# Centring the first expert weights during the first image steps, with the loads of both expert weights in the other order

## The reference

```python
x = x + _L0_conv_ref(_ln_c(x), ...)      # per image: a 3x3 convolution whose taps depend on the image
t = _to_tokens(x)
t = t + _L0_ffn_ref(_ln_t(t), ...)
...
def _L0_ffn_ref(x, Wg, bg, W1, b1, W2, b2):
    gate_logits = xf @ Wg + bg
    top_w, top_i = jax.lax.top_k(gate_logits, 2)
    ...
    for e in range(E):
        h = jax.nn.gelu(xf @ W1[e] + b1[e], approximate=False)
        out = out + w_dense[:, e:e + 1] * (h @ W2[e] + b2[e])
```

## Time and profile before

| | |
|---|---|
| median of three runs | 1544.35 us |
| the profiled execution | 1543.75 us, of which the span from first to last instruction is 1541.5 us |
| busy share of the span | TensorE 94%, VectorE 86%, ScalarE 71%, GpSimd 63% |
| first phase, up to the choice of the last pair | 0 to 570 us |
| turn between the phases | 570 to 611 us |
| second phase | 611 to 1541 us |
| granted TensorE clock, mean | 0.961 of full speed |

### The profile page before, as it was taken

The page is one execution under the profiler, slowest core; times in us unless marked ns, Lnnn a source line. Parts: engine busy times, 40 slices in busy tenths (PEclk is TensorE's granted clock), DMA queues, the critical chain, the costliest instruction groups (busy, mean ns, idle before and its releaser), DMA issues.

```text
span 1541.5 us, 45757 instructions
## 1 busy us (share of the span) xinstructions
PE 1446.2 (94%) x12204; PEld 1114.9 (72%) x12205; DVE 1326.2 (86%) x2693; ACT 1096.8 (71%) x2514; POOL 973.6 (63%) x1057
## 2 busy tenths in 40 slices
PE   5899999999999848999999999999999999999996
PEld 2345444454545422999999999999999999999995
DVE  2568888888888885999999999989999999999995
ACT  4577777777777622777777777777777777777773
POOL 1004455554555476577777777777777777777773
PEclk7899999999999955999999999999999999999998
DMA  4201212121222026111111223222322222222223
GB/s 140 82 28 57 69 62 79 64 74 56 73 69 65 31 83 138 47 45 43 44 40 55 68 86 92 88 93 86 92 86 91 86 91 86 90 81 82 75 78 108
DMA packets 85647, 115.77 MB, mean 75 GB/s; under 512 B 17613, under 2 KB 69865, under 8 KB 85590
## 3 DMA queue, kind: packets, MB, share of 16 engines
q1 hardware_dynamic: 64886, 76.83, 16.9%
q0 software_dynamic: 18112, 34.27, 6.8%
q10 hardware_dynamic: 2592, 4.00, 0.9%
HBM read 60.08 MB, written 58.48 MB: 77 GB/s over the span
## 4 chain that ended last, share of the span: by engine, by line
POOL 36%; PE 25%; issue 25%; ACT 8%; DVE 2%; POOLq 2%; DMA 1%; SPq 0%; DVEq 0%; ACTq 0%
POOL token_out L532 15%; POOL xn L520 13%; PE psV L860 12%; POOL yt L527 8%; PE psV L811 4%; ACT spent L628 3%; PE psT L845 2%; PE psA L802 2%; PE psG L847 2%; ACT cv L616 1%; ACT sq L584 1%; DMA stage<-in_L_ffn_W_dram 1%; POOLq L532 1%; DVE x L1174 1%; ACT lnv L591 1%
## 5 line engine op out<-in xcount | busy, mean ns | idle before, releaser
L1390 DVE TENSOR_TENSOR gl<-g,gh 128x512 f16<-128x512 f32 x620 | 497.6, 841 | 62.4 <-ACT gh L739 54.8
L502 POOL DMA_INDIRECT rows_by_pair<-rows,idx x256 | 269.2, 1052 | 325.4 <-issue 201.9
L532 POOL DMA_INDIRECT token_out<-yt,rt x310 | 354.5, 1144 | 185.0 <-POOL yt L527 132.7
L860 PE MATMUL psV<-lp,diag 128*128 128x512 f32 x576 | 275.1, 610 | 18.7 <-ACT cv L616 17.6
L739 ACT ACTIVATE gh<-g 128x512 f16<-128x512 f32 x465 | 274.5, 624 | 16.9
L732 ACT ACTIVATE g<-psT 128x512 f32<-128x512 f32 x310 | 182.0, 597 | 100.9 <-PE psT L996 61.0
L732 ACT ACTIVATE g<-psV 128x512 f32<-128x512 f32 x310 | 184.8, 598 | 90.1 <-PE psV L996 68.7
L520 POOL TENSOR_SCALAR xn<-rt 128x128 f32<-128x128 f32 x310 | 217.1, 709 | 9.4 <-DMA rt<-rows_by_pair 5.6
L1017 PE MATMUL psR<-wall,gh 128*128 x1240 | 221.3, 273 | 0.4 <-DVE ya L1407 0.4
L1017 PE MATMUL psG<-wall,gh 128*128 x1240 | 221.3, 273 | 0.0
L1018 PE MATMUL psG<-wall,gl 128*128 x1240 | 213.0, 219 | 0.0
(11 more groups left out here) (224 smaller groups left out, 2958.5 us busy)
## 6 DMA issues: line engine op xcount, KB each, us to landing
rt<-rows_by_pair SPq DMA_DIRECT2D x155, 133.0 KB
xb<-in_x_dram SPq DMA_DIRECT2D x32, 512.0 KB, 3.4
yq<-token_out SPq DMA_DIRECT2D x112, 128.0 KB, 2.3
out_dram<-oq SPq DMA_DIRECT2D x112, 128.0 KB
token_out<-yt,rt POOLq DMA_INDIRECT x310
rows_by_pair<-rows,idx POOLq DMA_INDIRECT x256, 2.4
stage<-in_L_ffn_W_dram SPq DMA_DIRECT2D x1, 2048.0 KB, 8.8
ye<-token_out SPq DMA_DIRECT2D x4, 512.0 KB, 4.1
```

The source lines that it names most:

```text
L502: gp.indirect_dma_start(rows_dram, bass.IndirectOffsetOnAxis(ap=idx[p][:, b:b + 1].bitcast(U32), axis=0), rows[p][:, b, :], None).then_inc ...
L532: gp.indirect_dma_start(y_dram, bass.IndirectOffsetOnAxis(ap=rt[r][:, b, ID:ID + 1].bitcast(U32), axis=0), yt[r][:, b, :], None, bounds_ch ...
L860: ins = te.matmul(psConv.rearrange("p (h w) -> p h w", w=WW), diag[k][:, m, :], lp[j][:, y:y + HH // 2, dx:dx + WW], start=(m == 0), stop= ...
L1390: v.tensor_tensor(gl[side][q][:, cols], g[side][:, cols], gh[side][q][:, cols], ALU.subtract).then_inc(lo_done, 1)
```

## The change

The loads change places, and W1 is made ready during the image steps:

- SP loads W1 at the place of W2's load; the wait and the load behind it are gone.
- TensorE multiplies W1 with `centre_w` (the identity less the mean) in place of the ones, so that the bank holds the centred weights, and adds b1 / 128 with the same second matmul. There are three banks (both halves of `psT` and `psG`); an expert from the fourth on waits until the bank's low part is read. Experts 0 to 2 stand at the end of step 0, 3 to 5 in the middle of step 1, 6 and 7 at the end of step 1.
- ScalarE makes the high part from the bank (three experts and b2 in the first half of step 1, three after the second square of step 1, two at the start of step 2), then issues the load of W2.
- VectorE makes the low part from the bank (three after the first norm of step 1, three before the second, two in step 2 after the first window taps).
- `turn` of step 2, which uses `psT` and `psG`, waits until all eight low parts are made.
- W2 is split by ScalarE in step 3 (four experts in the middle, four at its end) and by VectorE at the ends of steps 3 and 4. `low_b2` moves from step 0 to the end of step 1.
- The shift products, the shift, the high and the low parts between the phases are gone.

```diff
@@ SP
-            sp.dma_start(stage_2, W2.rearrange("e (s p) d -> p e s d", p=P)).then_inc(s_stage, 16)
+            sp.dma_start(stage_1, W1.rearrange("e d h -> d e h")).then_inc(s_stage, 16)
...
-            sp.wait_ge(s_low, 1)
-            sp.dma_start(stage_1, W1.rearrange("e d h -> d e h")).then_inc(s_stage, 16)
@@ ScalarE
+            def high_w1(part):
+
+                for e in range(*W1_PARTS[part]):
+                    act.wait_ge(s_w1_centred, e + 1)
+                    sc_.activation(wall_e[:, e, O_1H:O_1L], w1_bank[e % 3], ACT.Copy, scale=WSCALE).then_inc(s_w1_high, 1)
...
+                if st_.is_step(2):
+                    high_w1(2)
+                    act.dma_start(stage_2, W2.rearrange("e (s p) d -> p e s d", p=P)).then_inc(s_stage, 16)
                 if st_.on(2):
                     diagonals(st_, 0)
...
-                    if st_.first and k == 1:
-                        high_w2(E - 2, E)
+                    if k == 0 and st_.is_step(1):
+                        high_b2()
+                        high_w1(0)
                     if st_.on(1):
                         inv_std(st_, k, 1)
...
-                    if st_.first and k == 1:
-                        high_b2()
...
-                    if st_.first and k == 0:
-                        high_w2(0, E // 2)
                     if st_.on(1):
                         if k == 0:
                             square(st_, 1)
-                    if st_.first and k == 0:
-                        high_w2(E // 2, E - 2)
+                    if k == 0 and st_.is_step(1):
+                        high_w1(1)
+                    if k == 0 and st_.is_step(3):
+                        high_w2(0, E // 2)
                 if st_.next().on(1):
                     square(st_.next(), 0)
+                if st_.is_step(3):
+                    high_w2(E // 2, E)
...
-            for e in range(E):
-                act.wait_ge(s_shifted, e + 1)
-                sc_.activation(wall_e[:, e, O_1H:O_1L], stage_1[:, e, :], ACT.Copy, scale=WSCALE).then_inc(s_high, 1)
@@ TensorE
+            def centre_w1(part):
+
+                if part == 0:
+                    pe.wait_ge(s_stage, 16)
+                    pe.wait_ge(s_b1, 1)
+                for e in range(*W1_PARTS[part]):
+                    if e >= 3:
+                        pe.wait_ge(s_w1_low, e - 2)
+                    te.matmul(w1_bank[e % 3], centre_w[:, :], stage_1[:, e, :], start=True, stop=False)
+                    te.matmul(w1_bank[e % 3], ident[0:E, e:e + 1].broadcast_to([E, P]), b1n[:, :], start=False, stop=True).then_inc(s_w1_centred, 1)
...
                 pe.wait_ge(x1_ready, st_.count(3, 2, k + 1))
+                if k == 0 and st_.is_step(2):
+                    pe.wait_ge(s_w1_low, E)
...
+                    if k == 0 and st_.is_step(1):
+                        centre_w1(1)
...
+                for part, at in ((0, 0), (2, 1)):
+                    if st_.is_step(at):
+                        centre_w1(part)
...
-            for e in range(E):
-                te.matmul(shift_bank[e], ones[:, :], stage_1[:, e, :], start=True, stop=False)
-                te.matmul(shift_bank[e], ident[0:E, e:e + 1].broadcast_to([E, P]), b1n[:, :], start=False, stop=True).then_inc(s_shift, 1)
-
             pe.wait_ge(tab_ready, 2)
-            pe.wait_ge(s_shifted, 2)
...
-            pe.wait_ge(s_low, 2 + E)
+            pe.wait_ge(s_low, 2)
@@ VectorE
+            def low_w1(part):
+
+                for e in range(*W1_PARTS[part]):
+                    dve.wait_ge(s_w1_high, e + 1)
+                    v.scalar_tensor_tensor(out=wall_e[:, e, O_1L:O_2], in0=w1_bank[e % 3], scalar=WSCALE, in1=wall_e[:, e, O_1H:O_1L], op0=ALU.mult, op1=ALU.subtract).then_inc(s_w1_low, 1)
...
+                if st_.is_step(2):
+                    low_w1(2)
                 if st_.on(1):
                     norm(st_, 0)
...
-                    low_w2(0, E // 2)
+                if st_.is_step(1):
+                    low_w1(0)
...
                     window(st_, 2, 0, 0, 3)
+                if st_.is_step(1):
+                    low_w1(1)
                 if st_.on(1):
                     norm(st_, 1)
...
                     add_image(st_, 1)
-                if st_.first:
+                if st_.is_step(1):
+                    low_b2()
+                if st_.is_step(3):
+                    low_w2(0, E // 2)
+                if st_.is_step(4):
                     low_w2(E // 2, E)
-                    low_b2()
...
-            for e in range(E):
-                dve.wait_ge(s_shift, e + 1)
-                v.scalar_tensor_tensor(out=stage_1[:, e, :], in0=shift_bank[e], scalar=-1.0 / D, in1=stage_1[:, e, :], op0=ALU.mult, op1=ALU.add).then_inc(s_shifted, 1)
...
-            for e in range(E):
-                dve.wait_ge(s_high, 2 + e + 1)
-                v.scalar_tensor_tensor(out=wall_e[:, e, O_1L:O_2], in0=stage_1[:, e, :], scalar=WSCALE, in1=wall_e[:, e, O_1H:O_1L], op0=ALU.mult, op1=ALU.subtract).then_inc(s_low, 1)
```

More of the change, by code:

```diff
@@ L180, in conv_moe_block @@
         s_high, s_low = sem("weights_high"), sem("weights_low")
-        s_shift, s_shifted = sem("shift_products"), sem("weights_shifted")
+        s_w1_centred, s_w1_high, s_w1_low = sem("w1_centred"), sem("w1_high"), sem("w1_low")
         s_setup_pe = sem("setup_products")
@@ L296, in __init__, with is_step @@
                 self.first = self.fixed and t + r == 0
+            def is_step(self, n):
+                return self.fixed and 2 * self.t + self.r == n
             def on(self, stage):
@@ L335, in conv_moe_block @@
         ybank = (psG, psR)
-        shift_bank = [bank[:, half:half + H] for bank in (psA, psV, psT) for half in (0, 512)] + [psG[:, :], psR[:, :]]
+        w1_bank = [psT[:, 0:H], psT[:, 512:512 + H], psG[:, 0:H]]
+        W1_PARTS = ((0, 3), (3, 6), (6, E))
         HT = HS * T // 2
@@ L569, in high_w2 @@
                 if first == 0:
-                    act.wait_ge(s_stage, 16)
+                    act.wait_ge(s_stage, 32)
                 for e in range(first, end):
@@ L928, in step @@
                         tap_logits(st_, quarter)
+                for part, at in ((0, 0), (2, 1)):
+                    if st_.is_step(at):
+                        centre_w1(part)
             run_steps(pe, step)
-            pe.wait_ge(s_stage, 32)
-            pe.wait_ge(s_b1, 1)
             pe.wait_ge(cv_ready, 2 * NIMG)
@@ L1098, in gate_weights @@
                 v.tensor_tensor(cbd[:, :], cb[:, 1, :], cb[:, 0, :], ALU.subtract)
-                v.tensor_scalar(b1n[:, :], b1r[:, :], -1.0, None, ALU.mult).then_inc(s_b1, 1)
+                v.tensor_scalar(b1n[:, :], b1r[:, :], 1.0 / D, None, ALU.mult).then_inc(s_b1, 1)
                 v.memset(wgc[:, E:G], 1.0 / D)
```

## The result

The changed kernel takes 1568.2 us, the median of four runs, against 1544.75 of the kernel before in the same comparison: 1.0156 times, interval 1.0142 to 1.0171. The four times lie in two pairs, 1565.1 and 1565.6, 1570.9 and 1571.0. All runs of the changed kernel on record, these four and the six of the first experiment, have a median of 1570.4. The first profile is of the run of 1565.6 (span 1562.8, mean granted clock 0.959); a profile of a run of the upper pair came with the experiments.

The account below looks back on a forecast made before the run. Image steps were taken as a chain through TensorE and ScalarE with little cover; between phases GpSimd's scatters bound. 3.0 + 13.7 + 5.1 - 2.2 = +19.6 us on 1544.35 gives 1564; range 1554 to 1573.

Parts of the forecast that it names:

- the forecast: Whole kernel: +19.6 us, 1564, with the clock risen before the weights' products in step 0 and staying up; chance 0.47.
- the first rival: Steps 0 and 1: clock stays cold, three experts take 12.0 instead of 6.0 us; +26.6, 1571; chance 0.27.
- step 0: Image start: without W2's split ScalarE squares at 19.45, and the first variance runs at full clock; -4.5 us.
- step 2: TensorE's turn waits for VectorE's last low parts (+9.6), then runs at half clock (4.1); +13.7 us.
- Step 1's +3.0: Step 1's end: ScalarE's copy 1.9 us early, then three more experts' products add 4.9; 3.0 us late.
- rival 2: Step 2's wait costs less: clock survives the pause, or step 1 ends on time; +9 to +13, 1554 to 1557; chance 0.18.
- Steps 3 and 4: W2's split on ScalarE and VectorE delays convolution, norm and turn; +5.1 us, bounds 1.7 and 7.
- The 3.8: Step 4: the second image's turn starts at 153.7 instead of 149.93, delayed by the split and low parts; +3.8 us.
- the 1.3: Step 4's four low parts (2.49 us) make norm 2.3 late and the turn after it 1.3 us late.
- The turn between the phases: Between phases: SP's row loads start 0.9 us earlier, GpSimd's first normalisation is shorter; -2.2 us, bounds 0.9 and 2.5.
- rival 3: Image steps catch up the start's losses by the last scatters while the gains stay; 1538, faster; chance 0.04.
- rival 4: Change does next to nothing: low parts come before the taps, steps 3 and 4 absorb the split; 1545; chance 0.04.

Follow-up runs that it names:

- the first experiment: The changed kernel run again, unaltered, to see why its times fall into two groups: 1566.1, 1566.8, 1573.7, 1575.0, then 1570.3 and 1570.5 us.
- run of 1570.3: The changed kernel, unaltered, in a later profiled repeat: 1570.3 us.
- full_rows_after: Changed kernel with the second matmul of each expert reading 128 rows (b1 and zeros) instead of 8: 1566.8 us median, 1.0150.
- low_first: Changed kernel with step 2's last two W1 low parts ahead of the window taps and b2's low part a step later: 1560.4 us median, 1.0097.
- low_full: Changed kernel with step 2's two low parts ahead of the taps, b2's a step later, and 128 rows in each second matmul: 1555.4 us, 1.0068.
- upper group: The slower runs of the changed kernel, unaltered: 1570.3 to 1575.0 us, against runs near 1565.5 us.
- full_rows_before: Kernel before with 128 rows instead of 8 in each expert's second matmul between the phases: 1546.2 us, 1.0015.
- late_full_landed: Kernel before with W2's split at step 0's end, 128 rows, and low parts waiting until all scatters but two landed: 1536.2 us median, 0.9948.

## Why the prediction was right, point by point

The time lies in the range, the sign is right, and the median of 1568.2 stands between the forecast, 1564, and the first rival, 1571, because two of the four runs do the one and two the other; that it fell so near the forecast is luck, for the median of all ten, 1570.4, lies at the rival's time. By its own terms, each column from the ruler and the spans (1541.5 before, 1562.8 and 1568.3 after), in us:

| term | predicted | run of 1565.6 | run of 1570.3 |
|---|---|---|---|
| step 0 | -4.5 | -4.7 | -7.0 |
| step 1 ends late by | +3.0 | +3.1 | +7.6 |
| step 2 | +13.7 | +14.3 | +13.0 |
| split in steps 3 to 5 | +5.1 | +5.3 | +10.3 |
| steps 6 to 15 | 0 | +0.1 | +0.1 |
| last step to the end | -2.2 | -1.5 | -4.3 |
| sum (without step 0, which is in step 1's end) | +19.6 | +21.3 | +26.8 |

**Step 0** was right to 0.2 us in the run of 1565.6, square and clock: ScalarE's square was put at 19.45 and came at 19.46.

**Step 1's +3.0 was right by two errors that cancel.** The forecast let the clock rise before the weights' products and stay. It rose, at about 33 us, but fell again behind them, and a variance and four convolution records ran at half clock. On the other side ScalarE was to take back 2.0 us with b2 and three experts; in this run its copy of the convolution starts as the convolution ends (47.67, 47.64), 1.9 ahead of the 49.53 of before, as forecast, but because the convolution is late. In full_rows_after, in which the clock stays up, the copy starts at 45.74, 0.9 behind the convolution's end (44.80): so ScalarE takes back 0.9 and not 2.0. With the clock up and products of eight rows the copy would come some 2.8 early and not 1.9, an estimate from these rows: 3.8, less the 1.0 by which the 128 rows bring the variance behind the products forward (38.62, 39.66). An expert's products were put at 2.0 and took 2.1.

**Step 2 was right in its wait, and about right in the size of its half clock; the cause given for that is enough, but not the only one.** The turn stood at 84.97 where 72.37 plus 3.0 plus 9.6 gives 84.97. The half clock was put at 4.1 and cost 4.8 in this run (14.3 less 9.5, the turn's 12.6 without step 1's 3.1), some 4.2 by the experiments. The prediction named the pause as the cause, and in the changed kernel the clock does fall in it, near 80.8 us, with the variance ahead of it (77.55) still at full clock; full_rows_after shows that the pause alone is enough. What the prediction didn't see is that a shorter pause would not have saved the clock: low_first shows the fall without a pause, low_full none with 128 rows. So rival 2's door was shut twice. Its price was also added up wrongly: without 4.1 and 3.0 the sum is +12.5, without one of them +15.5 or +16.6, and nothing in it gives +9.

**Steps 3 and 4** were right in sum and in shape. The 3.8 was worked out at the norm and the second turn of step 4, so on the ruler it is the loss of steps 3 and 4 together, 3.7 (2.1 and 1.6); the 1.3 is that of step 5, 1.6. The norm of step 4 came 4.3 later than step 2's end alone makes it (163.63 less 141.91 and 17.4), where 4.6 was put. What the prediction had no term for is that the clock can fall in or behind the waits opened there (1.34, 1.95 and 1.40 us of TensorE; none over 1.2 us stood in these steps before), which in some runs takes a step from 33.1 to 34.8 or 36.4 us (in low_first, full_rows_after and low_full as well as in the upper group). In low_first's profile this gave back nearly all of the 6.1 us won in step 2.

**The turn between the phases** gave 1.5 us, where 2.2 were worked out. From the last scatter on it is 2.6 (that scatter is 23.9 later, the end 21.3); 1.1 is lost ahead of it, between the last exponential and the scatters. In the run of 1570.3 it is 2.7 from the last scatter on, and ahead of it 1.6 are gained. So the turn itself is alike in both, just over the upper bound of 2.5; of what varies ahead of it no experiment shows the cause. The mechanism, the table's wait and the low parts beside GpSimd's first normalisation, is the one that full_rows_before and late_full_landed bear out.

**The rivals.** The first, half clock through the products of step 0, is what both profiled runs of the upper group do, and six of the ten runs lie in that group: 1571 was worked out, 1570.3 to 1575.0 measured. Its parts were off (step 1 late by 7.6 and not 10, steps 3 to 5 by 10.3 and not 5.1, the end by -4.3 and not -2.2), and that the sum was not is luck. Nor did the clock stay cold from the start: it was up till 24.8 us and fell before the products. The rival's event came, an expert at 4.0 us, and its chance of 0.27 was low. Catching up (rival 3) and next to nothing (rival 4) fall by the ruler: +22.7 at step 5, +22.8 at step 15.

## What to carry to other kernels

Work that looks long in a stretch may lie beside something longer; ask what is late next before moving it, and price the place it moves to by the queue it enters: here 32 us of products gave back some 2.6 us, and a wait for two operations queued behind another stage's taps cost 6. Where a change opens a pause on TensorE or puts products of few rows between full ones, price the half clock behind it as a term of its own, and expect that it varies from run to run. When an operation finishes early after a repair, look at what it now runs beside: the low parts, made early, held up one of GpSimd's scatters by 3.8 us and cost more than the repair had won.

## What the runs showed of the hardware that was not expected

- Products with eight rows between ones with 128 are not cheaper than 128 rows in both, and here they are dearer: at a granted clock of 1.00 three experts took 6.21 us (54.53 to 60.74) with eight rows in the second matmul, 5.15 (52.58 to 57.73) with 128. Both matmuls of a pair lengthen: in the changed kernel each starts 1.05 us behind the one before it, in full_rows_after 0.86. TensorE's timelines, first the one, then the other:

```profile
55.48 1.12 PE L837 MATMUL psT<-b1n,ident 8*128 8x512 f32 x2
56.53 1.13 PE L836 MATMUL psT<-stage,centre_w 128*128 128x512 f32 x2
```

```profile
53.43 1.02 PE L838 MATMUL psT<-b1n,ident 128*128 128x512 f32 x2
54.29 1.02 PE L837 MATMUL psT<-stage,centre_w 128*128 128x512 f32 x2
```

- The granted clock fell to 0.50 behind such products with TensorE busy throughout (at 40 us in both profiles of runs under 1567 us; at 77.4 in low_first) and stayed at 0.50 for 34 us of them; with 128 rows it didn't fall behind them, and between the phases it was at 0.99 to 1.00 from 575 us on. The fall isn't certain: behind the three experts at 54.53 to 60.74 the clock stayed up. The Trainium skill ("TensorE: Matmul & The Clock Gate", Part 1) says that sustained matmul activity releases the throttle. Here it depended on the matmuls: behind those of eight rows the clock fell or stayed down with TensorE busy, behind the same ones with 128 rows it didn't. No run separates the few rows from the later starts that come with them (1.05 against 0.86).
- A scatter on GpSimd that began 0.95 us behind the first of VectorE's eight low parts lasted till 0.85 behind the last of them, 4.78 instead of 0.97 us, alike in three runs; one that began 0.23 behind the first took 1.30.
- A semaphore raised by GpSimd's sequencer behind its scatters in program order was up over 11 us before the last of them began on GpSimd's timeline (589.36 and 600.47).
